# Cross-attention with a routed feed-forward layer: transposing the normalised inputs on VectorE and by DMA instead of on TensorE

## What is computed

```python
# ln: normalise over the features, times gain, plus bias
x = x + xattn(ctx_1024, layernorm(x))
x = x + ffn(layernorm(x))

# xattn, per batch: 16 heads of 64
xc  = ln(ctx); lat = ln(latents)
q   = lat @ Wq
k, v = split(concat([xc, lat]) @ Wkv)          # 256 keys per batch
out = softmax(q k^T / 8) v @ Wout

# ffn: every token goes to the expert e = argmax(x . centroid_e), 8 experts
y   = x + relu(ln_e(x) @ w1_e^T + b1_e) @ w2_e^T + b2_e
out = a * y + (1 - a) * x,  a = sigmoid(x . centroid_e)
```

## Time and profile before

| | |
|---|---|
| median of 3 runs | 1099.69 us (1099.62 to 1101.4) |
| time of the profiled execution | 1102.49 us |
| its span, first to last instruction | 1100.7 us |
| mean granted TensorE clock | 0.993 |
| busy share PE, DVE, ACT, POOL | 98%, 72%, 59%, 47% |
| attention stage | from 20.7 to about 836 us |
| feed-forward stage | the rest, 13.1 us a block |

### The profile page before, as it was taken

How to read it: one execution, slowest core, us unless ns; L and a number is a source line. 1 busy time by engine, 2 the same in 40 slices (tenths; PEclk the granted TensorE clock), 3 DMA queues, 4 the chain that set the end, 5 groups by cost and what they waited for, 6 DMA issues and landing times.

```text
span 1100.7 us, 24234 instructions
## 1 busy us (share of the span) xinstructions
PE 1073.5 (98%) x8620; PEld 961.9 (87%) x8620; DVE 789.6 (72%) x1845; ACT 650.1 (59%) x1819; POOL 519.8 (47%) x640
## 2 busy tenths in 40 slices
PE   7899999999999999999999999999999999999995
PEld 5689888989888888889898888889898999999994
DVE  6785888887878888887988788887876553333331
ACT  5674666575756666665757566675566545455550
POOL 1563555455554455554555544555345443323331
PEclk9998999999999999999999999999999999999998
DMA  5464666565757566665658575664368466566550
GB/s 178 115 169 115 160 172 158 155 167 127 205 128 180 142 161 161 171 161 150 171 127 205 128 177 141 164 164 116 92 189 252 167 217 210 192 243 208 198 176 23
DMA packets 144109, 179.78 MB, mean 163 GB/s; under 512 B 15725, under 2 KB 133485, under 8 KB 139120
## 3 DMA queue, kind: packets, MB, share of 16 engines
q1 hardware_dynamic: 139536, 168.33, 56.1%
q0 software_dynamic: 3360, 8.53, 2.1%
q10 hardware_dynamic: 1088, 1.31, 0.3%
HBM read 65.72 MB, written 46.07 MB: 102 GB/s over the span
## 4 chain that ended last, share of the span: by engine, by line
PE 93%; DVE 2%; POOL 1%; DMA 1%; ACT 1%; issue 1%; SPq 0%; ACTq 0%; POOLq 0%; DVEq 0%
PE psum L635 16%; PE psum L668 15%; PE psum L810 12%; PE psum L705 10%; PE psum L795 9%; PE psum L684 9%; PE psum L720 8%; PE psum L654 8%; PE psum L595 1%; PE psum L723 1%; PE psum L763 1%; DMA w_ring<-in_w_q 1%; POOL prob L1519 1%; DMA prob_t<-prob 1%; DVE neg_max L1176 0%
## 5 line engine op out<-in xcount | busy, mean ns | idle before, releaser
L1519 POOL TENSOR_TENSOR prob<-prob,inv_sum 128x512 f32<-128x512 f32 x176 | 182.8, 1050 | 188.4 <-DVE inv_sum L1182 188.4
L948 ACT ACTIVATE prob<-psum,neg_max 128x256 f32<-128x256 f32 x352 | 162.9, 472 | 51.3 <-DVE neg_max L1176 42.9
L1176 DVE TENSOR_REDUCE neg_max<-psum 128x2 f32<-128x512 f32 x256 | 162.3, 674 | 35.5 <-PE psum L684 30.3
L810 PE MATMUL psum<-w,v_n 128*128 128x256 f32 x608 | 134.2, 379 | 0.0
L1188 DVE STREAM_TRANSPOSE prob<-prob 128x512 f32<-128x512 f32 x176 | 121.5, 699 | 9.1 <-POOL prob L1519 8.7
L810 PEld LDWEIGHTS psum<-w,v_n 128*128 128x128 f32 x608 | 114.1, 190 | 14.8
L1590 POOL DMA_INDIRECT out<-x_in,r_ring x38 | 48.9, 1286 | 149.6 <-DVE x_in L1393 143.8
L1519 POOL TENSOR_TENSOR w_ring<-w_ring,inv_sum 128x512 f32<-128x512 f32 x76 | 78.2, 1039 | 67.6 <-DVE inv_sum L1182 67.6
L955 ACT ACTIVATE head_out_hi<-psum 128x512 fp32r<-128x512 f32 x52 | 31.1, 598 | 128.2 <-PE psum L705 128.2
L927 ACT ACTIVATE k_hi<-psum 128x512 fp32r<-128x512 f32 x128 | 77.1, 603 | 35.2 <-PE psum L635 32.5
L938 ACT ACTIVATE v_n<-psum 128x512 f32<-128x512 f32 x128 | 77.1, 602 | 29.0 <-PE psum L668 29.0
(11 more groups left out here) (181 smaller groups left out, 2711.6 us busy)
## 6 DMA issues: line engine op xcount, KB each, us to landing
sorted_rows<-filler SPq DMA_DIRECT2D x54, 660.0 KB
prob_t<-prob SPq DMA_DIRECT2D x176, 128.0 KB, 2.7
w_ring<-prob SPq DMA_DIRECT2D x176, 128.0 KB, 3.0
w<-in_experts SPq DMA_DIRECT2D x19, 1024.0 KB
w_ring<-in_experts SPq DMA_DIRECT2D x18, 1024.0 KB
prob_t<-w_ring SPq DMA_DIRECT2D x76, 128.0 KB, 2.7
w_ring<-w_ring SPq DMA_DIRECT2D x76, 128.0 KB, 3.0
r_ring<-sorted_rows SPq DMA_DIRECT2D x19, 264.0 KB, 2.8
```

What stands on the lines that cost most here:

```text
L810: last = pe.matmul(bank[:, i * d_model:(i + 1) * d_model], hid[:, s % 2, f, i * P:(i + 1) * P], w2[:, f * d_model:(f + 1) * d_model], star ...
L948: act.activation(prob_at(u, bb)[:, :, parity, i], scores_i, ACT.Exp, bias=neg_max[:, at, i:i + 1], accum_out=prob_sum[:, at, i:i + 1]).the ...
L1176: dve.tensor_reduce(neg_max[:, (4 * u + n) % 8, :], psum[:, n, :].rearrange("p (i j) -> p i j", i=2), AXIS_X, ALU.max, negate=True).then_i ...
L1519: pool.tensor_tensor(probs, probs, inverse, ALU.mult).then_inc(s_soft, 1)
```

## The change

For all pairs from the third on, the normalised inputs no longer pass through TensorE. ScalarE's `normalise` writes them with the columns reordered (it reads every fourth column of its source, 64 at a time), VectorE transposes `normed` in 32x32 blocks (two instructions for a pair, at the end of its step r = 0), SyncE issues four DMAs of 128 KB that put the blocks in place, in a free half of `w1_ring` (at the head of its step r = 1), and ScalarE's `gain_bias_moved` reads them there. Gain and bias, the high and the low half of a side are done in r = 1 and 2 in place of r = 0 and 1. The work banks lose their 28 ("ln", g, side) turns. `places` of a pair's first batch goes from r = 0 to r = 1, and its `scatter` from r = 1 to r = 2; the reading of the ranks' bank stays in r = 0, as `read_ranks`.

```diff
@@ bank_order
-        order += [("ln", pair, side) for pair, side in inputs_of(u, n_pairs)]
+        order += [("ln", pair, side) for pair, side in inputs_of(u, n_pairs) if pair == 1]
@@ inputs_of
-    if u < 4:
+    if g == 0:
         return [(1, side) for side in range(2)] * (u == 2)
-    return [(g + 1, r)] if r < 2 and g + 1 < n_pairs else []
+    return [(g + 1, r - 1)] if r in (1, 2) and g + 1 < n_pairs else []
...
+            normed_blocks = normed[:].rearrange("p n d -> p (n d)").rearrange("p (j s b c k) -> p j s b c k", j=4, s=2, b=2, c=KC)
+            normed_cols = w1_ring[:, 0, KC * half:].rearrange("p (a s b c t) -> p a s b c t", a=4, s=2, b=2, c=KC)
+            def wait_inputs_moved(eng, g):
+                eng.wait_ge(s_moved[g % 2], 4 * 16 * (g // 2))
@@ SyncE
+                def move_inputs(g):
+                    sp.wait_ge(s_nrm_t, 2 * (g - 1))
+                    if g == 2:
+                        wait_made(sp, ("cent",))
+                    else:
+                        sp.wait_ge(s_y, 2 * (g - 2))
+                    for a in range(4):
+                        sp.dma_start(normed_cols[:, a].rearrange("p s b c t -> p (s b c t)"),
+                                     normed_blocks[a * Q:(a + 1) * Q].rearrange("p j s b c t -> p j (s b c t)")
+                                     ).then_inc(s_moved[g % 2], 16)
                 for u in range(n_steps + 1):
                     g, r = divmod(u, 4)
+                    if r == 1 and 1 <= g < n_pairs - 1:
+                        move_inputs(g + 1)
                     if u > 0:
                         move_probabilities(u - 1, 1)
...
                     if u == n_steps - 3:
                         wait_landed(sp, n_steps - 5, 1)
+                        sp.wait_ge(s_y, 2 * (n_pairs - 2))
                         load_weights_1(0)
@@ TensorE
                     for pair, side in inputs_of(u, n_pairs):
-                        normed_t(pair, side)
+                        if pair == 1:
+                            normed_t(pair, side)
@@ ScalarE
-                    if g >= 1:
+                    if g >= 3:
+                        wait_inputs_moved(act, g - 1)
+                    elif g >= 1:
                         wait_made(act, ("ln", g - 1, 1))
...
-                        last = act.activation(normed[:, j, :], src, ACT.Identity,
+                        dst = normed[:, j, :]
+                        if g >= 2:
+                            src = src.rearrange("p (c k j) -> p j c k", c=KC, j=4)
+                            dst = normed_blocks[:, :, side, j % 2]
+                        last = act.activation(dst, src, ACT.Identity,
                                               bias=ln_shift[:, g % 2, j:j + 1], scale=ln_scale[:, g % 2, j:j + 1])
...
+                def gain_bias_moved(g, side):
+                    wait_inputs_moved(act, g)
+                    wait_low(act, g - 1, side)
+                    for c in range(KC):
+                        last = act.activation(y_t[:, c, :, side * P:(side + 1) * P].rearrange("p b (a t) -> p b a t", a=4),
+                                              normed_cols[:, :, side, :, c, :].rearrange("p a b t -> p b a t"), ACT.Identity,
+                                              bias=ln_w[:, 2 * side + 1, c:c + 1], scale=ln_w[:, 2 * side, c:c + 1])
+                    last.then_inc(s_y, 1)
...
-                        gain_bias(pair, side)
+                        if pair == 1:
+                            gain_bias(pair, side)
+                        else:
+                            gain_bias_moved(pair, side)
@@ VectorE
+                def transpose_inputs(g):
+                    dve.wait_ge(s_nrm, g + 1)
+                    for h in range(2):
+                        half_of = normed[:, 2 * h:2 * h + 2, :].rearrange("p n d -> p (n d)")
+                        dve.transpose(half_of, half_of).then_inc(s_nrm_t, 1)
...
+                def read_ranks(g):
+                    item = ("rank", g)
+                    wait_made(dve, item)
+                    if g >= 1:
+                        dve.wait_ge(s_pos, 2 * g)
+                    last_reads(item, dve.tensor_tensor(place_2[:], work_bank(number[item])[:, 0:2 * n_experts]
...
                 def places(b):
-                    item = ("rank", b // 2)
+                    wait_read(dve, ("rank", b // 2))
...
+                    if r == 0 and 1 <= g < n_pairs - 1:
+                        transpose_inputs(g + 1)
...
                     if r == 0 and g >= 2:
-                        places(2 * g - 4)
+                        read_ranks(g - 2)
...
                     if r == 1 and g >= 2:
+                        places(2 * g - 4)
                         places(2 * g - 3)
@@ GpSimd
-                    if r == 1 and g >= 2:
+                    if r == 2 and g >= 2:
                         scatter(2 * g - 4)
+                        scatter(2 * g - 3)
                     if r == 2 and g >= 1:
                         row_scales(2 * g - 2)
-                    if r == 2 and g >= 2:
-                        scatter(2 * g - 3)
```

More of the change, by code:

```diff
@@ L225, in build @@
             s_nrm_x = sem("s_nrm_x")
+            s_nrm_t = sem("s_nrm_t")
+            s_moved = [sem("s_moved0"), sem("s_moved1")]
+            s_y = sem("s_y")
             s_var = sem("s_var")
@@ L989, in normalise_rows @@
                     if s < 2:
-                        wait_made(act, ("ln", n_pairs - 1, 1))
+                        wait_inputs_moved(act, n_pairs - 1)
                     else:
@@ L1188, in transpose_blocks @@
                     dve.transpose(probs, probs).then_inc(s_quad, 1)
+                def transpose_inputs(g):
[3 more added lines that the diff above has]
+                        dve.transpose(half_of, half_of).then_inc(s_nrm_t, 1)
                 def high_inputs(g, side):
-                    wait_read(dve, ("ln", g, side))
+                    if g == 1:
+                        wait_read(dve, ("ln", g, side))
+                    else:
+                        dve.wait_ge(s_y, 2 * (g - 2) + side + 1)
                     slot, part = 2 * (g % 2), slice(side * P, (side + 1) * P)
@@ L1269, in choose @@
                     dve.wait_ge(s_oh, b + 1)
+                def read_ranks(g):
[4 more added lines that the diff above has]
+                    last_reads(item, dve.tensor_tensor(place_2[:], work_bank(number[item])[:, 0:2 * n_experts]
+                                                      .rearrange("p (b e) -> p b e", b=2),
+                                                      tables[:, None, TAB_REGION:TAB_REGION + n_experts]
+                                                      .to_broadcast([P, 2, n_experts]), ALU.add))
                 def places(b):
-                    item = ("rank", b // 2)
+                    wait_read(dve, ("rank", b // 2))
                     row = row_ring[:, b % NROW, :]
-                    if b % 2 == 0:
-                        wait_made(dve, item)
-                        last_reads(item, dve.tensor_tensor(place_2[:], work_bank(number[item])[:, 0:2 * n_experts]
-                                                          .rearrange("p (b e) -> p b e", b=2),
-                                                          tables[:, None, TAB_REGION:TAB_REGION + n_experts]
-                                                          .to_broadcast([P, 2, n_experts]), ALU.add))
-                        wait_read(dve, item)
                     dve.tensor_copy(row.bitcast(I32)[:, COL_TOKEN:COL_TOKEN + 1], tables[:, TAB_TOKEN + b:TAB_TOKEN + b + 1])
@@ L1476, in _ @@
                 low_outputs(n_steps - 2)
+                read_ranks(n_pairs - 2)
                 places(n_batches - 4)
@@ L1491, in _ @@
                 finish(1)
+                read_ranks(n_pairs - 1)
                 places(n_batches - 2)
```

## The result

The changed kernel takes 1091.19 us (median of 6 runs, 1088.28 to 1094.01), the kernel before beside it 1100.47 us (6 runs, 1099.59 to 1104.54). The ratio is 0.9909, with a 95% interval from 0.9885 to 0.9934: faster by 0.9%. In a second set of six runs, beside runs of the kernel before, the same kernel gave 0.9886 (0.9866 to 0.9905). The forecast was 1087.0 us, which is 0.9885 of 1099.69.

A forecast was written before the change was run, and what follows sets the result against it. TensorE was taken to bound the kernel: 14 pairs x 0.91 us = 12.7 us off the median of 1099.7, all additions hidden, gives 1087.0 us. Own range 1085.5 to 1088.5 (chance 0.72); 1083 to 1092 holds some 0.83.

The forecast's parts named there:

- TensorE as the bound, 0.91 us a pair: Attention steps r = 0 and r = 1 lose 0.46 and 0.45 us of transposes; 12.7 us over 14 pairs.
- The strided read at nothing: ScalarE's normalisation reading every fourth column from SBUF costs nothing extra; other end 2.5 us a pair.
- rival 1: Slow strided read in ScalarE's normalisation, 2.5 us a pair; 0 to 14 us lost, 1087 to 1101; chance 0.13.
- The landing at T + 6.2 and a wait of 1.0 us: In r = 1, inputs land 6.2 us after T, the step's score start; ScalarE waits 1.0 us (0 to 1.6).
- VectorE's slack of 0.90 us in r = 1: VectorE's spare time in r = 1: 0.08 us behind `places`, 0.82 us ahead of the next maxima.
- The bound at T + 8.0: In r = 1, TensorE waits from T + 5.2 + 0.9 + 1.9 on; each later microsecond goes to TensorE.
- rival 3: Moves land late in r = 1, TensorE waits; landing at T + 10 costs 15 us: 1115 us; chance 0.06.
- GpSimd and the shifts at nothing: Both scatters at the head of r = 2, where GpSimd idles 3.00 us, and shifted `places` cost nothing.
- Rival 2: Clock drop from 84.4 to 91.2 us, around the centroid products, vanishes: 3.4 us less, 1083.6 us; chance 0.05.
- Rivals 1, 3 and 4: The last: step 32 held by something else, such as the probabilities' landing; no gain, 1099.7 us; chance 0.04.

The follow-up runs named there:

- Sides only: Kernel before with both sides of the next pair's inputs taken a step later, still transposed by TensorE; 1101.78 us, ratio 1.0.
- nothing instead: Changed kernel without VectorE's transposes and the four moves, gain and bias reading untransposed inputs; 1102.1 us with one more feed-forward block, steps 6 to 63 706.99 us.
- the straight read: Changed kernel with `normalise` reading without a stride, columns in another order; 1101.81 us with one more feed-forward block, steps 6 to 63 706.99 us.
- The repeat: The changed kernel run once more, unaltered; 1089.46 us, ratio 0.9886 to the kernel before.
- moves last: Changed kernel with SyncE issuing the inputs' moves behind the probabilities of r = 1; 1124.91 us, ratio 1.0215 to the kernel before.
- places only: Kernel before with only the shift of `places` and `scatter` a step later; 1102.31 us, ratio 0.9998.

## Why the prediction was right, point by point

**TensorE as the bound, 0.91 us a pair: right.** 11.78 us over 13 pairs is 0.906 us, and the fourteenth gave 0.93 to 0.96 us. Together 12.7 us, the sum of the prediction. Sides only showed that it moves with the instructions, nothing instead that nothing of it was lost to the new path.

**The strided read at nothing: wrong.** This is the step that failed. I took the price from the exponential on PSUM, which reads at the same stride, and kept SBUF's own behaviour as the other end. It is 0.85 us against 0.61 us for 256 elements, 0.25 us an instruction and 1.0 us a pair, between the two ends of 0 and 2.5 us. The page "SBUF — State Buffer" of the Trainium skill, section "Door 1: The DMA port swizzle", had the direction: an access to a new 16-byte line pays. A row on PSUM was no row on SBUF. It had no effect on the time: the steps are the same with the straight read. That was luck as far as this step of the forecast goes, which had no sum for a read that costs 1.0 us a pair; rival 1 had one only for 2.5 us. By its sum ScalarE would enter r = 0 later by 1.0 - 0.30 = 0.7 us, and the landing stays short of the bound.

**The landing at T + 6.2 and a wait of 1.0 us: mis-sized.** Measured T + 7.2 and 1.88 us, past the 1.6 of the range. The failed term is SyncE's. I had the moves go out from T + 0.1 to T + 2.6, on the ground that the cast's absence lets the probabilities ahead of them start 0.68 us earlier. They start at T - 3.08, as in the kernel before (T - 3.06), and take 3.38 us, not 2.71. VectorE's timeline shows what holds them now:

```profile
434.29 0.71 DVE L1233 STREAM_TRANSPOSE prob<-prob 128x512 f32<-128x512 f32 x1 [0.29 <-POOL prob L1583]
```

The transpose ahead of their issue waits for GpSimd's scaling, so what the cast gave back is not passed on. Then come the two loads, then four moves in 3.56 us and not 2.5. The slow read has its share: with the straight one these probabilities go out at T - 3.35, and the wait shrinks by 0.35 to 0.4 us a pair. Why issues of moves are longer in these places, with one of a pair's four at up to 1.67 us, no run isolates.

**VectorE's slack of 0.90 us in r = 1: too low by some 0.6 us.** In the first trace's step 33 it took `y_t` 2.08 us later against T than before (T + 8.33, after T + 6.25), and its next maxima came 1.18 us later: 0.90 us were absorbed, but 0.57 us of idle time stand in between that no row explains. The repeat has the same step without them (its steps 33 and 34 start at 433.90 and 447.80):

```profile
442.56 0.43 DVE L1248 CAST kv_t_hi<-y_t 128x512 fp32r<-128x512 f32 x1 [2.62 <-ACT y_t L949]
...
449.68 1.25 DVE L1221 TENSOR_REDUCE neg_max<-psum 128x2 f32<-128x512 f32 x2
```

`y_t` is taken at T + 8.66, 2.41 us later, and the maxima come 1.88 us into their step, 0.87 us later: 1.54 us are absorbed. Of the 0.64 us more than forecast, the cast of the first side gives 0.49 (0.43 us, not 0.92) and `places` 0.08 (0.62 us, not 0.70).

**The bound at T + 8.0: 0.5 us too early**, with the rule of one for one right, as moves last shows. With VectorE's slack as measured, the prediction's own sum is 5.2 + 1.5 + 1.9 = T + 8.6, against T + 8.5. The loss came by two ways, of which I had one. The 6.9 us from issue to landing that rival 3 names go with T + 8.9; with the last move issued at T + 2.0, as forecast, a landing at T + 10 needs 8.0 us.

**GpSimd and the shifts at nothing: right**, by places only and sides only.

**The time: 1087.0 forecast, 1091.19 and 1089.46 measured.** Both medians lie above the forecast's own range of 1085.5 to 1088.5, and inside the wider 1083 to 1092. The pairs gave what was forecast. By ratio it is 0.9885 forecast, 0.9909 and 0.9886 measured: 9.3 and 13.4 us of gain between the medians, with 12.7 forecast. In the first trace the span fell by 10.9 us: 11.30 and 0.96 in the steps, less 1.25 at the start, 0.14 in steps 0 to 3 and 0.03 at the end. The start differs between runs of kernels that share it (19.75 and 20.71 before, 22.59 in sides only, with 6.83 us at 1.2 GHz from 10.2 us on), so that loss is no price of the change. And the kernel before itself had medians of 1099.69 to 1102.82 us in its sets of runs. What made the first set's gain smaller in its other five runs stays open, as only one of them has a trace. **Rival 2**, the clock coming back, did not happen: the drop was there in both traces of the changed kernel, 6.83 and 3.41 us long. **Rivals 1, 3 and 4** are out: the slow read was true, but its loss was hidden; TensorE had no waits.

## What to carry to other kernels

Two like steps of the same trace, one with the work and one without it, price the removal of work from the bounding engine to a hundredth of a microsecond, as long as the waits say that it is the bound. For what is added, write down until when each result may be late and by whom it is wanted, and follow every engine's list behind the late one; that bound was worth more here than the exact landing, which I missed by 1 us. Idle time ahead of an instruction is slack only if the instruction starts as early as its inputs allow; compare its start with the step's start first. Price an access pattern from a row of the same memory, and give it both ends where there is none.

## What was not expected of the hardware

- ScalarE reading 128x256 float32 from SBUF at every fourth element takes 0.85 us, straight 0.61 us. From PSUM the exponential at the same stride takes 0.472 us and the ReLU reading straight 0.481 us; these are two functions, so the comparison is a rough one.
- The stretches at 1.2 GHz were 3.41 or 6.83 us long in every trace (the kernel's end left out), one or the other by the run. They began at 10 to 11 us, at 33 to 38 us, and at 81 to 86 us in or behind the products for the centroids. In steps 4 and 5 of one kernel the long one costs 1.5 us more than the short one (32.55 against 31.01 before, 31.59 against 30.08 after), and step 0 started 1.0 and 2.2 us apart between two traces of one kernel. To tell a change of 3 us, compare traces by their steps.
- The same cast of 128x512 took 0.43 us on VectorE where GpSimd stood idle, and 0.92 us in the kernel before where GpSimd was scaling probabilities from 448.02 to 450.05 us beside it. This holds for all of them from 78 us on. In the changed kernel's trace 12 of 28 such casts ran with GpSimd idle and took 0.43 us each; the other 16 overlapped with one of its operations and took 0.56 to 1.25 us, each about 0.3 us more than the overlap. In the kernel before all 28 overlapped, and none took less than 0.91 us. After step 33's cast GpSimd starts only when the cast is done:

```profile
446.94 1.30 POOL L1576 TENSOR_TENSOR kv_t_lo<-y_t,kv_t_hi 128x512 fp32r<-128x512 f32 x1 [1.95 <-DVE kv_t_hi L1248]
```
